# TensorE's order of sums in a split state-space scan: the second tile's read-out is summed ahead of the first tile's

## The reference

```
def step(h, inp):
    d_t, b_t, c_t, u_t = inp
    h = h * jnp.exp(d_t[:, :, None] * A) + (d_t * u_t)[:, :, None] * b_t[:, None, :]
    y = jnp.einsum('bdn,bn->bd', h, c_t)
    return (h, y)
...
y = ys.swapaxes(0, 1) + u * D_param
y = y * _silu(z)
return jnp.einsum('bld,ed->ble', y, out_proj_w)
```

## Time and profile before

| | |
|---|---|
| median of 3 runs | 2833.23 us (2825.04 to 2836.41) |
| the profiled execution, its own time | 2836.86 us |
| its span | 2835.1 us |
| PE, DVE, ACT, POOL busy | 87%, 63%, 50%, 17% |
| mean granted TensorE clock | 0.91 |

### The profile page before, as it was taken

How to read it: one execution, slowest core, us unless ns; L and a number is a source line. 1 busy time by engine, 2 the same in 40 slices (tenths; PEclk the granted TensorE clock), 3 DMA queues, 4 the chain that set the end, 5 groups by cost and what they waited for, 6 DMA issues and landing times. The chain is left out here.

```text
span 2835.1 us, 39198 instructions
## 1 busy us (share of the span) xinstructions
PE 2458.7 (87%) x13340; PEld 1096.7 (39%) x13340; DVE 1798.2 (63%) x4325; ACT 1431.1 (50%) x2576; POOL 491.1 (17%) x618
## 2 busy tenths in 40 slices
PE   6799999999999999999678798976778996999858
PEld 4333334343433434333243323435444533433235
DVE  3686777777777777777237775357868234878333
ACT  2365666666666666666535033247454421566510
POOL 1210111110111111010014001005666001200010
PEclk8799999999999999999889898988889995999858
DMA  2231222222222222121010000003332002221120
GB/s 85 81 94 46 82 66 69 72 79 59 70 65 78 69 63 84 50 70 54 20 36 1 22 1 27 0 13 141 119 114 102 29 20 82 79 76 58 37 95 15
DMA packets 77457, 171.68 MB, mean 61 GB/s; under 512 B 23050, under 2 KB 38666, under 8 KB 73164
## 3 DMA queue, kind: packets, MB, share of 16 engines
q1 hardware_dynamic: 77258, 169.18, 18.8%
HBM read 128.41 MB, written 39.71 MB: 59 GB/s over the span
## 5 line engine op out<-in xcount | busy, mean ns | idle before, releaser
L1056 ACT ACTIVATE sb_prob<-ps 128x512 f32<-128x512 f32 (+1 forms) x1520 | 805.7, 575 | 483.2 <-PE ps L846 307.5
L820 PE MATMUL ps<-sb_k_stack_half,sb_q_stack_half 78*128 78x512 bf16 (+3 forms) x1920 | 588.2, 340 | 55.4 <-DMA sb_q_stack_half<-q_rows 23.6
L846 PE MATMUL ps<-sb_q_stack_half,sb_k_stack_half 81*128 81x128 bf16 (+2 forms) x2240 | 570.3, 312 | 53.5 <-ACT sb_prob L1056 51.9
L957 DVE TENSOR_REDUCE sb_row_max<-ps 128x1 f32<-128x512 f32 x640 | 431.9, 686 | 140.2 <-PE ps L820 138.3
L966 DVE CUSTOM_DVE_ANT_0 sb_masked_scores<-ps,sb_mask_row,sb_row_max 128x128 bf16<-128x128 f32 (+3 forms) x640 | 341.5, 544 | 93.8 <-PE ps L820 90.6
L966 DVE CUSTOM_DVE_ANT_0 sb_masked_scores<-ps,sb_mask_row 128x128 bf16<-128x128 f32 (+3 forms) x640 | 283.3, 487 | 171.9 <-PE ps L820 171.1
L846 PEld LDWEIGHTS ps<-sb_q_stack_half,sb_k_stack_half 81*128 81x128 bf16 x2240 | 201.7, 99 | 386.3 <-ACT sb_prob L1056 198.4
L867 PE MATMUL ps<-sb_prob,sb_v_first_half 128*9 128x512 f32 (+3 forms) x2560 | 300.9, 543 | 0.2 <-ACT sb_o_raw L1063 0.2
L820 PEld LDWEIGHTS ps<-sb_k_stack_half,sb_q_stack_half 78*128 78x128 bf16 x1920 | 184.5, 100 | 268.1 <-DVE sb_row_max L966 80.2
L2715 PE MATMUL ps<-sb_read_out,sb_ident 128*128 128x512 f32 x256 | 135.6, 680 | 54.2 <-DVE sb_read_out L2872 51.1
L1129 POOL CAST sb_max_parts<-sb_row_max 128x16 bf16<-128x16 f32 x80 | 15.7, 196 | 760.6 <-DVE sb_row_max L966 760.6
(11 more groups left out here) (384 smaller groups left out, 3616.1 us busy)
## 6 DMA issues: line engine op xcount, KB each, us to landing
sb_q_stack_half<-q_rows SPq DMA_DIRECT2D x240, 96.0 KB
sb_k_stack_half<-k_rows SPq DMA_DIRECT2D x40, 576.0 KB
o_rows<-sb_o_raw SPq DMA_DIRECT2D x80, 256.0 KB, 2.3
sb_b_spread<-b_rows SPq DMA_DIRECT2D x32, 512.0 KB, 4.4
sb_c_spread<-c_rows SPq DMA_DIRECT2D x32, 512.0 KB, 3.6
sb_k_stack_half<-k_rows SPq DMA_DIRECT2D x40, 288.0 KB
q_rows<-sb_qk_parts SPq DMA_DIRECT2D x60, 128.0 KB, 2.1
k_rows<-sb_qk_parts SPq DMA_DIRECT2D x60, 128.0 KB, 2.1
```

Of the source, the lines that this page charges most:

```text
L820: pe.matmul(M.ps[:, k % RING, 0:hi - lo], qst[half][0:S1_ROWS, s, j, at:at + P], kst[half][0:S1_ROWS, s, lo // CH, j, 0:hi - lo], start=Tr ...
L846: mm = pe.matmul(bank[:, x * w + lo:x * w + hi], kst[half][0:S2_ROWS, s, t // 4, j, t % 4 * P:(t % 4 + 1) * P], qst[half][0:S2_ROWS, s, j, ...
L957: dve.reduce_max(rowmax[:, tau % 3, 0, at:at + 1], M.ps[:, k % RING, 0:w], AX_X).then_inc(first_done, 1)
L1056: act.activation(prob[:, st % PROB_STEPS, heads[0]:heads[-1] + 1, a:CH], scores.rearrange("p (j q) -> p j q", j=len(heads)), ACT.Exp).then ...
```

## The change

In TensorE's list the two sums of a step change places. Nothing is added or removed, and no other engine's list is touched.

```
                         inflow(g)
+                        if g >= 2:
+                            gather(g - 2, 1)
                         if g:
                             gather(g - 1, 0)
-                        if g >= 2:
-                            gather(g - 2, 1)
                     gather(G - 2, 1)
                     gather(G - 1, 0)
                     gather(G - 1, 1)
```

## The result

Median 2805.59 us of 5 runs (2803.89 to 2812.28), against 2833.23 us of 5 runs of the kernel before (2825.04 to 2839.41): 27.6 us less. The ratio of the two is 0.9909, 95% interval [0.9885, 0.9933]. The profiled execution took 2803.89 us, its span is 33.0 us shorter than that of the earlier trace rows.

What follows compares the result with a forecast made beforehand. No engine filled the scan; a ring of waits among POOL, TensorE and DVE bound it. Gains and losses by stretch summed to 28.2 us, taking the median from 2833.2 to 2805 us, range 2795 to 2824.

Steps and rivals of the forecast that it cites:

- steps 1 to 3: Start of the scan: in step 3 DVE's product comes behind POOL's inflow; a loss of 0.7 us.
- steps 4 to 6: Scan stretch of 21.81 us: 6.4 us for the first step, twice 5.8 after; a gain of 3.8 us.
- steps 7 to 10: Scan stretch of 39.25 us: POOL's products take turns with DVE's softplus, making 46.1 us; a loss of 6.9 us.
- steps 16 and 17: Scan stretch of 20.91 us: tile 1's sum runs earlier, both totals follow the read-out at once; a gain of 7.2 us.
- steps 18 to 21: Scan stretch of 32.88 us holding the two products of L2843: comes to 30.0 us, a gain of 2.9 us.
- steps 22 to 30: Nine regular scan steps of 64.19 us: 5.8 us each, 52.2 us; a gain of 12.0 us.
- the tail: End of the scan, 14.00 us: POOL's last read-out need not wait behind two sums; a gain of 2.9 us.
- The ring: Regular scan steps: POOL's read-out waits for TensorE's sums, which wait for DVE's read-out; 7.36 us a step, 5.8 without it.
- A: Rival, 24%: DVE's read-out loses its meeting with POOL every second regular step; the gain falls to 14 us, 2819 us.
- B: Rival, 12%: in regular steps the meeting is lost nearly always; 28 us eat the gain, 2833 us.
- C: Rival, 5%: regular steps become TensorE's own at the lower clock, 10.05 us each; 2865 us if all 14 are so.
- D: Rival, 9%: softplus and POOL take no turns in steps 7 to 10, nothing lost there; gain 35 us, 2798 us.

## Why the prediction was right, step by step

The sum was 28.2 us. The scan gained 28.9 (259.2 less 230.3), and the medians 27.6. That the median came within 1 us of the forecast is partly luck: the interval of the ratio alone leaves a gain of 19 to 33 us, and the scans compared are those of two single profiles with the same start. With the other start the old order would take 264 to 267 us (an estimate: the 261.5 of the run changed in step 17 alone, and the 5.3 that this saved, less up to 2.4 by which its steps from 18 on were longer) against some 230 in the new, a gain of 34 to 37.

| term | forecast | measured |
|---|---|---|
| steps 1 to 3 | -0.7 | -2.8 |
| steps 4 to 6 | +3.8 | +2.5 |
| steps 7 to 10 | -6.9 | -5.6 |
| steps 11 to 14 | +4.2 | +4.3 |
| step 15 | +2.8 | +2.8 |
| steps 16 and 17 | +7.2 | +7.3 |
| steps 18 to 21 | +2.9 | +4.8 |
| steps 22 to 30 | +12.0 | +12.6 |
| the tail | +2.9 | +3.0 |

*The ring.* Right, and shown by two independent ways to break it. The period after the change, taken from the one early step without a sum to wait for the earlier trace rows, was 5.81 us and came out as 5.73. The prediction's ring of 7.36 us is the whole step in only four of the nine steps before. The last four take 8.1 and 6.2 us in turn, 7.1 in the mean; there too POOL waits for the sums each time (3.4 and 0.55 us).

*The loss in steps 7 to 10.* Right in kind and near in size: the four steps took 14.7, 16.5, 5.5 and 8.2 us against 15.0, 17.2, 5.7 and 8.2. The run with POOL held shows as its cause that the products keep each other out. That the old order lost so little there (39.2 us) hung on its start: with the other start it took 43.2. *Steps 16 and 17.* Right; 5.3 to 5.4 of the 7.3 us are the order in step 17.

*Terms that were mis-sized.* The start was charged 0.7 and cost 2.8: that DVE's read-out would meet POOL (2.82 us) was seen, but not the two additions of step 3. They took 1.26 us before and 3.42 beside POOL's read-out:

```profile
1956.54 3.42 DVE L2891 TENSOR_SCALAR sb_step_one_plus<-sb_step_exp 128x1024 f32<-128x1024 f32 x2
```

With the other start the change costs only 0.5 us there (22.2 to 22.7). In steps 4 to 6 I had 6.4, 5.8 and 5.8 us; they took 5.5, 7.1 and 6.6, because ACT was 1.3 us late with the decay for step 6, and the read-out behind then took 2.3 us. In steps 18 to 21 I took step 21's meeting for lost (7.8 us), and it was won (6.3). These errors nearly cancel (-2.1, -1.3, +1.3 and +1.9), so the sum is better than its parts.

*The rivals.* A did not occur in the regular steps, but its mechanism is real and as near as was said: 0.07 us of lead, and 9.2 us lost when it is taken away. B and C did not occur: the granted clock went from 0.95 to 1.00 in steps 22 to 30. D is refuted by steps 7 to 10. The rule of the Trainium skill ("SBUF — State Buffer", "Who interferes with whom"), that whoever of VectorE and GpSimd issues first keeps the other out for a whole instruction, agrees with the meetings shown here: DVE won with leads from 0.04 us and lost when 0.04 us or more behind. The rows of the run with the clear fit it only if the clear counts as the first.

## What to carry to other kernels

When an engine that is little busy waits for another that is little busy too, look for the ring: list who releases whose buffer, and ask whether the release stands in a queue behind something that is not ready. An instruction whose input is a step old belongs in front of one whose input is just being made; a third buffer did most of the same for more memory (a scan of 236.5 us against 230.3). And once the ring is gone, look for what the freed engine now collides with: here its products got in the way of DVE's, and holding it back in two steps was worth some 10 us of the scan.

## What was not expected of the hardware

Without any work added, one semaphore wait on an engine's own previous instruction moved the next one by 0.1 us and, through the exclusion between DVE's and POOL's products, made four of nine steps 2.1 us longer and the others 0.2 (60.8 against 51.6 us for the nine). And the scan repeated to 0.02 us a stretch between two executions of the kernel before whose total times differed by 18 us, while the kernel changed in step 17 alone, with the same instructions up to there and the other start, took 4.9 us longer for steps 1 to 10 (86.4 against 81.5).
